# Graph network on one core: row arrivals counted in parts of two, and GpSimd waits for the last part but one

## The reference

```python
h = jnp.maximum(_layernorm(x), 0.0); x = x + layer0(h, edge_index, ...)   # four times, layers 0 to 3
# layer 0, attention:      p = exp(leaky_relu(a_s[src] + a_d[dst]) - m[dst])
#                          out = segment_sum(h[src] * p / denom[dst], dst) + bias
# layer 1, softmax:        logits = (Q[:, src] * K[:, dst]).sum(-1) / scale;  alpha = softmax(logits, axis=1)
#                          agg = segment_sum(Q[:, src] * alpha, dst), 4 heads; then norm, gate, two linear maps
# layer 2, filter:         m = linear(h)[src] * ssp(linear(ssp(linear(edge_attr))));  agg = segment_sum(m, dst)
# layer 3, mixed sum:      h = x + segment_sum(x[src], dst);  out = relu(h @ W1 + b1) @ W2 + b2
```

## Time and profile before

| | us |
|---|---|
| Median of 3 runs | 5824.28 (5824.12 to 5836.3) |
| Profiled execution, its own time | 5816.28 |
| Its span | 5814.5 |
| TensorE busy | 3950.5 (68%) |
| GpSimd busy | 2882.5 (50%) |
| VectorE busy | 2150.8 (37%) |
| ScalarE busy | 1347.4 (23%) |

### The profile page before, as it was taken

The page is one execution under the profiler, slowest core; times in us unless marked ns, Lnnn a source line. Parts: engine busy times, 40 slices in busy tenths (PEclk is TensorE's granted clock), DMA queues, the critical chain, the costliest instruction groups (busy, mean ns, idle before and its releaser), DMA issues. The chain is left out here.

```text
span 5814.5 us, 74722 instructions
## 1 busy us (share of the span) xinstructions
PE 3950.5 (68%) x20694; PEld 3212.8 (55%) x20695; DVE 2150.8 (37%) x6441; ACT 1347.4 (23%) x1886; POOL 2882.5 (50%) x3007
## 2 busy tenths in 40 slices
PE   3655556667667777767677766666666663888888
PEld 1645555557546666666667644444444442666666
DVE  4932222223534333333335622222222244323232
ACT  1000000000221000000003544444444453323222
POOL 3866566662235555555551155555555545555551
PEclk7555555555665555555557866666666675888888
DMA  4521111110332222222221222222222222111111
GB/s 122 175 56 42 42 43 43 42 42 19 100 110 58 53 55 54 55 53 56 54 54 45 73 77 72 72 72 73 72 72 71 73 63 80 37 36 35 35 36 35
DMA packets 256054, 357.31 MB, mean 61 GB/s; under 512 B 52798, under 2 KB 179189, under 8 KB 255861
## 3 DMA queue, kind: packets, MB, share of 16 engines
q0 software_dynamic: 90624, 185.78, 12.5%
q1 hardware_dynamic: 165241, 169.55, 9.9%
HBM read 316.13 MB, written 39.00 MB: 61 GB/s over the span
## 5 line engine op out<-in xcount | busy, mean ns | idle before, releaser
L787 POOL DMA_INDIRECT m_rows<-table,m_idx x1568 | 1494.9, 953 | 1092.4 <-issue 464.6
L787 POOL DMA_INDIRECT m_rows<-table,e_idx x464 | 442.4, 954 | 365.3 <-DVEq L1312 172.1
L787 POOL DMA_INDIRECT m_more<-table,e_idx x480 | 453.6, 945 | 294.6 <-DVEq L1056 158.4
L1077 PE MATMUL e_agg<-e_weights,m_more 128*128 128x16 f32 x1152 | 339.4, 375 | 297.7 <-DMA lo_dram<-su_lob 193.7
L1513 PE MATMUL e_z<-e_w,e_filt 128*128 128x128 f32 x1568 | 375.4, 399 | 183.3 <-issue 180.7
L1077 PEld LDWEIGHTS e_agg<-e_weights,m_more 128*128 128x128 f32 x1152 | 311.3, 330 | 323.4 <-issue 323.2
L1078 PE MATMUL e_agg<-e_weights,m_ones 128*128 128x32 f32 x1568 | 481.3, 400 | 3.9 <-issue 3.9
L1513 PEld LDWEIGHTS e_z<-e_w,e_filt 128*128 128x128 f32 x1568 | 322.3, 293 | 267.1 <-issue 266.7
L1502 PE MATMUL e_z<-e_edge,e_w 128*128 128x512 f32 x392 | 290.8, 882 | 261.5 <-DVEq L1582 240.9
L1400 PE MATMUL e_out<-e_counts,e_nodes 128*128 128x256 bf16 x2964 | 444.6, 306 | 24.7 <-issue 24.4
L1746 PE MATMUL e_agg<-e_weights,m_rows 128*128 128x64 f32 x1568 | 356.4, 421 | 124.3 <-DVE e_weights L1863 79.8
(11 more groups left out here) (304 smaller groups left out, 6683.0 us busy)
## 6 DMA issues: line engine op xcount, KB each, us to landing
e_edge<-edge_T SPq DMA_DIRECT2D x98, 512.0 KB
lu_place<-lo_dram SPq DMA_DIRECT2D x49, 512.0 KB
m_rows<-table,m_idx POOLq DMA_INDIRECT x1568
e_key<-key_dram SPq DMA_DIRECT2D x98, 256.0 KB
key_dram<-key_out SPq DMA_DIRECT2D x13, 1024.0 KB
table<-m_rows SPq DMA_DIRECT2D x39, 256.0 KB, 2.3
m_more<-table,e_idx POOLq DMA_INDIRECT x480
m_rows<-table,e_idx POOLq DMA_INDIRECT x464
```

Source lines behind the costliest of these rows:

```text
L787: pool.indirect_dma_start(rows[:, t, :], None, table, bass.IndirectOffsetOnAxis(ap=idx[:, t:t + 1], axis=0)).then_inc(arrived, 16)
L1077: pe.matmul(to[:, 0, cols], s.rows[at.r][:, t, :], both[:, t, 0, :], start=False, stop=False)
```

## The change

Each row buffer gets `PARTS = 4` arrival semaphores in place of one, each for two gathers; in the attention stage ("the first pass") it is two, each for four gathers. Consumers wait for all of a buffer's semaphores, through `wait_rows`. GpSimd's gathers go through `gather_paced`: before part q it waits until part q-2 has landed, and for the first two parts of a chunk until the last two parts of the previous buffer have (not for the first buffer of a turn of the ring or of a round). Each such wait is followed by a `sem_inc` on `idx_seen`. `gather_straight` counts by halves and waits for nothing.

```diff
+PARTS = 4
+def wait_rows(eng, landed, uses):
+    for part in landed:
+        eng.wait_ge(part, uses * (16 * C // len(landed)))
+def gather_part(pool, rows, idx, landed, table, q):
+    per = C // len(landed)
+    for t in range(q * per, (q + 1) * per):
         pool.indirect_dma_start(rows[:, t, :], None, table, bass.IndirectOffsetOnAxis(ap=idx[:, t:t + 1], axis=0)
-                                ).then_inc(arrived, 16)
+                                ).then_inc(landed[q], 16)
+def gather_paced(pool, rows, idx, landed, table, turn, seen, ahead=None):
+    parts = len(landed)
+    for q in range(parts):
+        if q >= 2:
+            pool.wait_ge(landed[q - 2], (turn + 1) * (16 * C // parts))
+            pool.sem_inc(seen, 1)
+        elif ahead is not None:
+            pool.wait_ge(ahead[q + parts - 2], (turn + 1) * (16 * C // parts))
+            pool.sem_inc(seen, 1)
+        gather_part(pool, rows, idx, landed, table, q)
...
@@ gather_in_order, one_turn (first_turn, gather_long_ring and mixed_sum_edges likewise)
-            gather_chunk(pool, m.rows[r], m.idx[b][:, r * C:(r + 1) * C], s.gathered[r], table)
+            gather_paced(pool, m.rows[r], m.idx[b][:, r * C:(r + 1) * C], s.gathered[r], table, turn, s.idx_seen,
+                         s.gathered[r - 1] if r else None)
...
@@ mixed_sum_edges, copy_next
-                            pool.wait_ge(s.gathered[GATHER * b + j], (at.half + at.b) * (16 * C))
+                            wait_rows(pool, s.gathered[GATHER * b + j], at.half + at.b)
...
@@ filter_edges, VectorE
-                        v.wait_ge(arrived(s, at), (at.turn + 1) * 16 * C)
+                        wait_rows(v, arrived(s, at), at.turn + 1)
...
@@ softmax_edges, turn_rows on TensorE
-                        pe.wait_ge(arrived(s, at), (at.turn + 1) * 16 * C)
+                        wait_rows(pe, arrived(s, at), at.turn + 1)
```

More of the change, by code:

```diff
@@ L781, in clear_bank, with gather_chunk @@
     pe.matmul(bank[:, 0:cols], m.zeros[:], m.zeros[:].unsqueeze(1).to_broadcast([1, cols // P, P]), start=True, stop=False)
[L784 to L788 removed]
+PARTS = 4
[5 more added lines that the diff above has]
+    for t in range(q * per, (q + 1) * per):
+        pool.indirect_dma_start(rows[:, t, :], None, table, bass.IndirectOffsetOnAxis(ap=idx[:, t:t + 1], axis=0)
+                                ).then_inc(landed[q], 16)
+def gather_chunk(pool, rows, idx, landed, table):
+    for q in range(len(landed)):
+        gather_part(pool, rows, idx, landed, table, q)
[8 more added lines that the diff above has]
+            pool.sem_inc(seen, 1)
+        gather_part(pool, rows, idx, landed, table, q)
 def turn_size(k, turn):
@@ L803, in early_semaphores @@
     early = Names()
-    early.gathered = [nc.alloc_semaphore(f"{name}gathered{r}") for r in range(RING)]
+    early.gathered = [[nc.alloc_semaphore(f"{name}gathered{r}_{q}") for q in range(PARTS)] for r in range(RING)]
     early.idx_ready = nc.alloc_semaphore(name + "idx_ready")
     early.idx_seen = nc.alloc_semaphore(name + "idx_seen")
-    early.all = early.gathered + [early.idx_ready, early.idx_seen]
+    early.all = sum(early.gathered, []) + [early.idx_ready, early.idx_seen]
     return early
@@ L815, in early_rows @@
     early.rows, early.begun = rows, begun
-    early.gathered = [nc.alloc_semaphore(f"{name}gathered{r}") for r in range(len(rows))]
+    early.gathered = [[nc.alloc_semaphore(f"{name}gathered{r}_{q}") for q in range(2)] for r in range(len(rows))]
     early.idx_loaded, early.dst_loaded = nc.alloc_semaphore(name + "idx_loaded"), nc.alloc_semaphore(name + "dst_loaded")
-    early.all = early.gathered + [early.idx_loaded, early.dst_loaded]
+    early.all = sum(early.gathered, []) + [early.idx_loaded, early.dst_loaded]
     return early
@@ L845, in gather_by_window @@
         for landed in s.early.gathered:
-            pool.wait_ge(landed, 16 * C)
+            wait_rows(pool, landed, 1)
             pool.sem_inc(s.idx_seen, 1)
@@ L905, in one_turn @@
                 copy(turn + 1, 1 - b, following)
-            gather_chunk(pool, s.rows[r], s.idx[b][:, r * C:(r + 1) * C], s.gathered[r], table)
+            gather_paced(pool, s.rows[r], s.idx[b][:, r * C:(r + 1) * C], s.gathered[r], table, turn, s.idx_seen,
+                         s.gathered[r - 1] if r else None)
     copy(1, 0, size(1))
@@ L1159, in mixed_sum_edges @@
         s.rows_free = [sem(f"rows_free{b}") for b in range(len(slots))]
-        s.gathered = [sem(f"gathered{b}") for b in range(len(slots))]
+        s.gathered = [[sem(f"gathered{b}_{q}") for q in range(PARTS)] for b in range(len(slots))]
         s.gathered_w = s.gathered
@@ L1182, in gather_round @@
                         r = GATHER * at.b + j
+                        ahead = s.gathered[r - 1] if j else None
                         pool.wait_ge(s.rows_free[r], at.half + 1)
@@ L1186, in gather_round @@
                             first = (at.n * ROUND + j) * C
-                            gather_chunk(pool, slots[r], m.src_idx[:, first:first + C], s.gathered[r], table)
+                            gather_paced(pool, slots[r], m.src_idx[:, first:first + C], s.gathered[r], table, at.half, s.idx_seen, ahead)
                         else:
```

24 lines of the change are left out of this document (12 added, 12 removed).

## The result

The changed kernel took 5786.3 us (median of 8 runs), the kernel before 5824.2 us in the same comparison. The ratio is 0.9936, with a 95% interval of 0.9913 to 0.9959. The forecast was no change, 5828 us. The profiled execution took 5775.61 us with a span of 5773.8, 40.7 us less than before's 5814.5.

A forecast was written before the change was run, and what follows sets the result against it. It held that no engine is full and a period is GpSimd's burst plus the consumers' work after it. 5816.28 + 0 + 4 + 0 = 5820, with the median's 8 us 5828; range 5434 to 5870.

The forecast's parts named there:

- Stalls set the period; without any, some 4530 us.: Edge stages: a period is GpSimd's burst plus consumers' work after it; no stall at all would save 1291 us.
- The 1190 waits on GpSimd find the rows landed and cost 0.: GpSimd, before gathers: each new wait with its count finds its rows landed and costs 0, as at a chunk boundary.
- 1.62: Landing of a chunk's last gather, read at TensorE's L1708: rows there at most 1.62 us after the record's end.
- the sum is 0 + 4 + 0: Whole kernel: GpSimd's waits 0, filter stage consumers' waits 4 us, other consumers' waits 0, added to the profiled 5816.28 us.
- the first rival: Edge stages: waits hold GpSimd back and stalls shrink, by some 50 to 390 us, 5774 to 5434 us; chance 0.34.
- The consumers' waits cost 4 us.: Filter stage, VectorE ahead of the release at L1595: three more waits per chunk, taken as 4 us, at most 25.
- priced at 0: Mixed sum, TensorE ahead of L1384: the consumers' added waits cost 0, at most 15 us.
- The second rival: GpSimd's parts get longer and stages pay in full; at 0.05 us a wait pair 42 us, 5866 us; chance 0.21.

The follow-up runs named there:

- a3: Changed kernel, but GpSimd waits before each part for the part four back, so waits never bind; without stalls, 1.0019 of the kernel before (4406.4 us).
- a2: Changed kernel with arrivals counted in parts but no wait on GpSimd for landings; without stalls, 0.9974 of the kernel before (4406.4 us).
- b1: The changed kernel again, unchanged, on another chip, with stalls; 1.0025 of the kernel before (5667.6 us).
- the control: The kernel before run again unchanged, with stalls, beside counting in parts alone; 0.9975 of the kernel before (5808.8 us).
- c4: Changed kernel, but GpSimd waits before each part for the last part; with stalls, 1.1701 of the kernel before (5808.8 us).
- d1: Changed kernel with two parts of four gathers in all stages, GpSimd waiting before each four for the last four; with stalls, 0.9758 of the kernel before (5812.2 us).
- d3: Changed kernel with one part of eight gathers, GpSimd waiting before each chunk for the last chunk's landing; with stalls, 0.9328 of the kernel before (5812.2 us).
- a4: Changed kernel, but GpSimd waits before each part for the last part; without stalls, 1.5379 of the kernel before (4406.4 us).
- f2: Changed kernel with parts of 3, 1, 3, 1 gathers (attention 7, 1), waiting only for the last 3 or 7; without stalls, 1.0992 of the kernel before (4408.3 us).
- f4: The kernel before with three register loads behind the fourth gather of each chunk; without stalls, 1.0001 of the kernel before (4408.3 us).
- a1: The kernel before run again, unchanged; it ran without stalls, 1.0005 of the kernel before (4406.4 us).

## Why the prediction was wrong

Its steps, in its order:

- *Stalls set the period; without any, some 4530 us.* Right, and the best part of it. The kernel without stalls takes 4405 us, and GpSimd's 10.0 us for a chunk is its bound, as priced. That such executions exist was not foreseen.
- *The 1190 waits on GpSimd find the rows landed and cost 0.* Here the prediction first goes wrong, in two ways. The price was read at a chunk boundary inside a burst (1.25 us from 406.38 to 407.63). Behind the copy of the indices the same wait and count delay the first gather by 0.09 us (0.54 us for 0.45), which puts a later gather into VectorE's L1898; without stalls that costs 19.5 us against counting alone (a3 and a2). And some fifty waits bind, because the landing takes GpSimd 2.36 us, at times 3.26, and not 1.62.
- *So nothing changes on GpSimd, and the sum is 0 + 4 + 0.* This is the step that failed. The terms were taken as small, and they were added to the time as they stood, with their own sign. With the stalls, the 0.45 us that a lengthened gather adds to a burst take 1.9 us off what follows (21 of 23 turns at 1.4 us each, some 30 us in the softmax stage), and a signal that comes just before a stall in place of just after it moves by 9 to 11 us (L1852, 66.1 us before, 12.8 after). The sum left out that edits of little cost shift gathers against VectorE's instructions and TensorE's signals. Counting in parts alone gave 0.9961 with stalls and 0.9974 without, where 4 us slower was forecast for it. Why b1 gains nothing stays open. That the kernel came out faster is not the first rival's doing either.
- *The consumers' waits cost 4 us.* In the filter stage no such cost can be seen: it is 22 us shorter with counting alone, for a reason that stays open. In the mixed sum, priced at 0, counting costs 10 us against the control, and the changed kernel 16 to 22, which is shown, but not which wait it is.
- *The first rival, fewer gathers under way shrink the stalls.* As a mechanism right (c4, d1 and d3 show it), for this change not: two parts under way are four gathers, and a landing of 2.4 us behind a record of 0.94 at a cadence of 1.25 is two to three under way anyway. The limit sits above what there is. VectorE's stall at L1876 even grew, to 444.4 us.
- *The second rival, longer parts lengthen the stall.* With the stalls refuted in sign: the one chunk of four whose burst got longer is the one that gained. Without them right in kind: a3 is 19.5 us longer than a2, by longer gathers.

The rule on back-pressure in the Trainium skill (DMA: Bandwidth & Descriptors, Back-pressure in remote DMA) says of transfers between cores that a saturated destination clogs the path, with 25 to 75 requests queued. The runs agree with a thing that fills while gathers come without a pause and empties in one. They don't agree with data that land late: in a4, without stalls, GpSimd goes on 2.35 us after a record's end in the median, and in d3, after eight gathers in a row and with stalls, 2.3 to 2.4 us. What is late are the engines' signals, and what is missing are records of updates.

What stays open: what fills, and whether it is the recording of semaphore updates; whether it takes a full drain (d1, d3) or any time without a gather (f2 and f4 were to tell); why some executions have none of it; why a lengthened gather ends a stall early; and where counting in parts gains in the filter stage.

## What to carry to other kernels

A limit on what is under way does something only below what is under way without it: from the cadence and the time to land one can work out that number (here two to three gathers) before choosing the limit (with a limit of four the stalls stayed; a drain each eight gathers brought 6.7%, each four 2.4%). Where engines stall in step with another's bursts, edits of next to no cost of their own move the time by some tenths of a per cent either way, so "no change" deserves less weight than the sum of small terms suggests. A cost of 0.09 us is worth asking what it shifts an instruction into. And a repair of such stalls should be timed where they are absent too: the drain that pays 6.7% with them wasn't run without, but shorter pauses (0.7 to 1.0 us) cost 5 to 10% there. When two runs of one program differ this much, count the records of the traces before explaining the difference.

## What the runs showed of the hardware

- The same program took 4405 to 4408 us in three comparisons and 5668 to 5824 us in the others, with all of its variants alike in each. Of the difference of 1411 us between two spans, 1357 are in the edge stages (836 for 1134 us, 1005 for 1383, 976 for 1377, 610 for 888); the phases before and between them differ by some 21 us or less each. The traces with the long times lack records of semaphore updates (25,724 for 65,348).
- A gather of 128 rows of 512 bytes is issued every 1.25 us, and GpSimd can go on from its landing 2.3 to 2.4 us after its record's end, with and without stalls; about one in ten takes 2.8 us or more (114 of 1109 in a4).
- A gather that starts while VectorE runs an instruction with two inputs of 128x512 (L1863, 0.69 us) or 128x1024 (L1592, 1.23 us) takes longer, the more of that instruction is left. In a1's filter stage it takes 1.93 us when it starts 0.1 us after L1592, 1.47 to 1.54 at 0.5 us, 1.05 to 1.14 at 0.9 us, and 0.94 from 1.1 us on: its record ends 2.0 us after L1592's start, wherever it began. One of them:

```profile
2656.59 1.23 DVE L1592 SCALAR_TENSOR_TENSOR e_message<-e_soft,m_rows 128x1024 f32<-128x1024 f32 x1 [0.24 <-DVE e_soft L1587]
2657.11 1.53 POOL L787 DMA_INDIRECT m_rows<-table,m_idx  x1 [0.30 <-issue]
```

- Four gathers in a row followed by 2.3 us without one didn't stall VectorE's L1876 once in 98 chunks; eight in a row with the same pause did, for 390.7 us in all.
